# One program part for experts and final sum, with the last four experts' results moved on TensorE

## What is computed

```python
logits = jnp.einsum('bsd,ed->bse', x, gate_w) + gate_b
probs = jax.nn.softmax(logits, axis=-2)
vals_t, idx_t = jax.lax.top_k(probs.transpose(0, 2, 1), K)
...
merged = jnp.einsum('bked,bke->bed', tok, vals)
...
h = jnp.einsum('bei,eih->beh', jnp.concatenate([merged, ones], -1), w1)
h = jax.nn.gelu(h, approximate=False)
o = jnp.einsum('bej,ejo->beo', jnp.concatenate([h, ones], -1), w2)
out_tok = jnp.einsum('beo,bke->bkeo', o, vals).reshape(b, K * E, d)
out = jnp.zeros_like(x).at[jnp.arange(b)[:, None], flat_idx].add(out_tok)
```

## Time and profile before

| | us |
|---|---|
| median of three runs (lowest, highest) | 877.07 (875.35, 880.38) |
| the profiled execution's own time | 874.81 |
| its span | 873.1 |
| TensorE busy (matmuls) | 706.8 |
| DVE busy | 614.8 |
| ACT busy | 355.5 |
| GpSimd (POOL) busy | 452.6 |

### The profile page before, as it was taken

How to read it: one execution, slowest core, us unless ns; L and a number is a source line. 1 busy time by engine, 2 the same in 40 slices (tenths; PEclk the granted TensorE clock), 3 DMA queues, 4 the chain that set the end, 5 groups by cost and what they waited for, 6 DMA issues and landing times. The chain is left out here.

```text
span 873.1 us, 20447 instructions
## 1 busy us (share of the span) xinstructions
PE 706.8 (81%) x7708; PEld 475.9 (55%) x7708; DVE 614.8 (70%) x889; ACT 355.5 (41%) x561; POOL 452.6 (52%) x257
## 2 busy tenths in 40 slices
PE   4566759886899999999999999994899859976774
PEld 3354534444677777777776777773677523322231
DVE  3599947888999999999999999993477520100014
ACT  2366635443445544455444545542555321210000
POOL 1598700001999999999999999993122000000000
PEclk9799979998999999999999999996999959889685
DMA  5100000000001010000000000001930188999987
GB/s 111 49 2 0 0 1 0 0 0 14 8 15 38 14 33 9 12 12 12 12 8 11 12 12 12 14 15 56 389 100 1 40 346 341 412 413 421 413 350 247
DMA packets 49211, 86.34 MB, mean 99 GB/s; under 512 B 5552, under 2 KB 32752, under 8 KB 49168
## 3 DMA queue, kind: packets, MB, share of 16 engines
q1 hardware_dynamic: 45616, 83.33, 26.1%
q10 hardware_dynamic: 3552, 2.43, 0.9%
HBM read 76.31 MB, written 9.44 MB: 98 GB/s over the span
## 5 line engine op out<-in xcount | busy, mean ns | idle before, releaser
L898 POOL TENSOR_TENSOR read<-state,q_pos 128x1024 f32<-128x1024 f32 x128 | 300.4, 2365 | 28.7 <-DVE state L1007 22.4
L1007 DVE TENSOR_TENSOR_SCAN state<-fac,ps_up 128x1024 f32<-128x1024 f32 x128 | 290.0, 2277 | 8.6 <-ACT fac L942 8.6
L942 ACT ACTIVATE fac<-ps_xf 128x1016 f32<-128x1016 f32 x128 | 130.2, 1018 | 176.3 <-PE ps_xf L1041 159.9
L1041 PE MATMUL ps_xf<-hot,xtab 64*128 64x128 f32 x2048 | 148.4, 284 | 11.0 <-ACT fac L942 8.9
L1041 PEld LDWEIGHTS ps_xf<-hot,xtab 64*128 64x128 f32 x2048 | 125.4, 188 | 58.0 <-ACT fac L942 43.8
L1041 PE MATMUL ps_up<-hot,utab 64*128 64x128 f32 x2048 | 139.9, 276 | 19.5 <-DVE state L1007 19.5
L1041 PEld LDWEIGHTS ps_up<-hot,utab 64*128 64x128 f32 x2048 | 126.4, 189 | 25.1 <-issue 17.8
L907 POOL TENSOR_TENSOR utab<-tab 128x1024 f32 (+1 forms) x32 | 64.5, 2016 | 93.8 <-SPq L85 93.8
L1086 PE MATMUL ps_o<-read,sel 128*32 128x256 f32 x1024 | 82.7, 395 | 3.7 <-POOL read L898 3.7
L1637 DVE COPY h_t<-ps_ht 128x512 f32<-128x512 f32 x16 | 10.3, 686 | 75.5 <-PE ps_ht L1666 75.4
L997 DVE TENSOR_TENSOR xtab<-tab,ps_k 128x1024 f32<-128x1024 f32 x64 | 59.5, 929 | 1.5 <-PE ps_k L1033 1.5
(11 more groups left out here) (199 smaller groups left out, 987.7 us busy)
## 6 DMA issues: line engine op xcount, KB each, us to landing
w_sb<-in_L_ffn_w SPq DMA_DIRECT2D x32, 2048.0 KB, 20.1
rec_out<-osb SPq DMA_DIRECT2D x128, 32.0 KB, 1.5
ao<-rec_out SPq DMA_DIRECT2D x8, 512.0 KB, 4.1
out_dram<-h SPq DMA_DIRECT2D x8, 256.0 KB, 2.5
out_dram<-h ACTq DMA_DIRECT2D x8, 256.0 KB, 3.1
tok<-in_x SPq DMA_DIRECT2D x2, 512.0 KB, 10.6
exp_out<-eo SPq DMA_DIRECT2D x8, 128.0 KB, 18.6
oq<-exp_out SPq DMA_DIRECT2D x8, 128.0 KB, 2.9
```

The lines of the kernel that those rows point to most:

```text
L898: nc.gpsimd.tensor_tensor(read[n % 2][:], state[n % 4][:].rearrange("p (b i t) -> p b i t", b=2, i=IB), q_pos[x.s][:, :, x.k].unsqueeze(2) ...
L942: nc.scalar.activation(fac[n % 2][:].rearrange("p (n t) -> p n t", t=T)[:, :, 1:], ps_x[:].rearrange("p (n t) -> p n t", t=T)[:, :, 1:], A ...
L1007: nc.vector.tensor_tensor_scan(state[n % 4][:], fac[n % 2][:], ps_u[n % 2][:], 0.0, ALU.mult, ALU.add)\
L1041: last = nc.tensor.matmul(dst[:, b * 512 + col * T:b * 512 + (col + 1) * T], stationary[rows], pos[rows], start=True, stop=True)
```

## The change

Experts and combine become one program part, and the parts share one Chain semaphore for DVE and one for GpSimd. The last four experts (set 7, LAST = 28 on) no longer go through DRAM:

- At the start GpSimd builds strip, from which picks_of_last takes selectors: TensorE, between first_layer(0, 0) and first_layer(0, 1), brings the last four experts' picks of quad q to partitions 32j + 8x + q, with zeros on the strip's other partitions, and DVE copies them to last_picks.
- At the end rows_of_last puts the last result (128 rows in eo) on the same partitions with four matmuls, and DVE copies them to last_rows.
- Set 6's result is stored from ACT's queue. ACT then waits for that store and for those of sets 0 to 5 (set 5's is still in SP's queue, after the last w2 loads), and issues the reload: four transfers of 28 partitions by eight quads, 224 KB each.
- The sum of a quad is now eight matmuls: four over 28 partitions, picks times oq, and four over 32, last_picks times last_rows.

PSUM is one tensor of eight banks, used by both stages. In the diff below, the other places where a chain's own semaphore gives way to the shared one are left out, as are lines that only move.

```diff
 HT = HID // P
+LAST = X - QB
 EPS = 1e-5
...
-        m = {"start": start}
+        m = {"start": start, "vch": Chain(nc.vector, sem("v_chain")), "pch": Chain(nc.gpsimd, sem("p_chain"))}
...
             recurrent_outputs(nc, a, m, sem, lambda n, s, d=F32: sb(mid, n, s, d), replace_tables)
-        m["oq"] = sb(life, "oq", [P, QUADS, E])
         with ExitStack() as last:
-            experts(nc, a, m, sem, lambda n, s, d=F32: sb(last, n, s, d))
-        combine(nc, m, sem, out)
+            experts(nc, a, m, sem, lambda n, s, d=F32: sb(last, n, s, d), out)
...
-            ch = Chain(dve, vch)
+            ch = m["vch"]
...
-        pch, ch = Chain(nc.gpsimd, sem("p_chain1")), Chain(nc.vector, sem("v_chain5"))
+        pch, ch = m["pch"], m["vch"]
...
-def experts(nc, a, m, sem, sb):
-
-    ident, merged, exp_out, oq = m["ident"], m["merged"], m["exp_out"], m["oq"]
+def experts(nc, a, m, sem, sb, out):
+
+
+    ident, merged, exp_out, h2, picked = m["ident"], m["merged"], m["exp_out"], m["h2"], m["picked"]
     w1, w2, b1, b2, w1_ld, w2_ld = m["w1_sb"], m["w2_sb"], m["b1_sb"], m["b2_sb"], m["w1_ld"], m["w2_ld"]
...
     eo = sb("eo", [P, 2, E])
+    oq = sb("oq", [P, QUADS, E])
+    last_rows = sb("last_rows", [P, E])
+    last_picks = sb("last_picks", [P, QUADS, T])
+    strip = sb("strip", [P, QUADS + X])
...
     with ExitStack() as ctx:
-        ps_1 = [ctx.enter_context(nc.psum_tensor(f"ps_1{s}", [P, HID], F32)) for s in range(2)]
-        ps_t = ctx.enter_context(nc.psum_tensor("ps_ht", [P, HT, P], F32))
-        ps_2 = [ctx.enter_context(nc.psum_tensor(f"ps_2{s}", [P, 512], F32)) for s in range(2)]
+        ps = ctx.enter_context(nc.psum_tensor("ps_e", [P, 8, 512], F32))
+        ps_1 = [ps[:, 2 * s:2 * s + 2].rearrange("p n c -> p (n c)") for s in range(2)]
+        ps_t = ps[:, 4:6].rearrange("p n (h q) -> p (n h) q", q=P)
+        ps_2 = [ps[:, 6 + s] for s in range(2)]
+        ps_q = [ps[:, 4 * s:4 * s + 4] for s in range(2)]
+        ps_p = ps[:, 4, 0:E]
...
         mq_ok, gl, ht, htok, eo_ok = (sem(n) for n in ("mq_ok", "gl", "ht", "htok", "eo_ok"))
-        l1, l2, eo_st, f_ld = ([sem(f"{n}{s}") for s in range(2)] for n in ("l1_", "l2_", "eo_st", "z_ld"))
-        m["f_ld"] = f_ld
+        l1, l2, eo_st, f_out = ([sem(f"{n}{s}") for s in range(2)] for n in ("l1_", "l2_", "eo_st", "z_out"))
+        sp_ok, lp_mm, lp_ok, lr_mm, lr_ok, f_ld, f_mm, f_add = (
+            sem(n) for n in ("sp_ok", "lp_mm", "lp_ok", "lr_mm", "lr_ok", "z_ld", "z_mm", "z_add"))
+        dst = out.rearrange("(q p s) t e -> q s t p e", s=2, p=2)
+
+        def store_rows(eng, s):
+            for q in range(QUADS):
+                eng.wait_ge(f_add, START + q + 1)
+                eng.dma_start(dst[q, s], h2[:, QB * q + 2 * s:QB * q + 2 * s + 2]).then_inc(f_out[s], 16)
+            eng.wait_ge(f_out[s], START + 16 * QUADS)
+
+        def store_results(eng, i, s):
+            q = 2 * i + s
+            eng.wait_ge(eo_ok, START + q + 1)
+            eng.dma_start(exp_out[bass.ds(QB * q, QB)].rearrange("x b e -> (x b) e"), eo[:, s]).then_inc(eo_st[s], 16)
         TURNS = X // QB // 2
...
             for s in range(2):
                 hidden(TURNS - 1, s)
 
+            store_results(act, TURNS - 1, 0)
+            act.wait_ge(eo_st[0], START + 16 * TURNS)
+            act.wait_ge(eo_st[1], START + 16 * (TURNS - 1))
+            src = exp_out.rearrange("x (q j) e -> j x q e", j=QB)
+            for j in range(QB):
+                act.dma_start(oq[j * X:j * X + LAST], src[j, 0:LAST]).then_inc(f_ld, 16)
+            store_rows(act, 1)
+
+        @block.gpsimd
+        def _(pool):
+            pch = m["pch"]
+            cols = strip[:].rearrange("p (x q) -> p q x", q=QUADS)[:, QUADS - 1, 0:QB]
+            pch.link(nc.gpsimd.memset(strip[:], 0.0))
+            pch.link(nc.gpsimd.tensor_tensor(cols, ident[:, LAST:X], ident[:, X + LAST:2 * X], ALU.add))
+            pch.link(nc.gpsimd.tensor_tensor(cols, cols, ident[:, 2 * X + LAST:3 * X], ALU.add))
+            nc.gpsimd.tensor_tensor(cols, cols, ident[:, 3 * X + LAST:4 * X], ALU.add).then_inc(sp_ok, 1)
+
         @block.sync
         def _(sp):
             m["start"](sp)
-
-            def store(i, s):
-
-                q = 2 * i + s
-                sp.wait_ge(eo_ok, START + q + 1)
-                sp.dma_start(exp_out[bass.ds(QB * q, QB)].rearrange("x b e -> (x b) e"),
-                             eo[:, s]).then_inc(eo_st[s], 16)
-
-            def reload(h):
-
-                quads = slice(h * QUADS // 2, (h + 1) * QUADS // 2)
-                src = exp_out.rearrange("x (q j) e -> j x q e", j=QB)
-                for j in range(QB):
-                    sp.dma_start(oq[j * X:(j + 1) * X, quads], src[j][:, quads]).then_inc(f_ld[h], 16)
...
                 for h in range(2):
                     sp.wait_ge(l2[s], START + 2 * i - 1 + h)
                     load_w2(sp, a, QB * (2 * i + s), h, w2[s], w2_ld[s])
-                store(i - 1, s)
+                store_results(sp, i - 1, s)
...
             for s in range(2):
                 second_weights(TURNS - 1, s)
-            for s in range(2):
-                store(TURNS - 1, s)
-            for s in range(2):
-                sp.wait_ge(eo_st[s], START + 16 * TURNS)
-            for h in range(2):
-                reload(h)
+            store_rows(sp, 0)
 
         @block.vector
         def _(dve):
+            dve.wait_ge(lp_mm, START + 1)
+            nc.vector.tensor_copy(last_picks[:], ps_t).then_inc(lp_ok, 1)
...
                     nc.vector.tensor_copy(eo[:, s], ps_2[s][:, 0:E]).then_inc(eo_ok, 1)
+
+            dve.wait_ge(lr_mm, START + 1)
+            nc.vector.tensor_copy(last_rows[:], ps_p).then_inc(lr_ok, 1)
+            for q in range(QUADS):
+                dve.wait_ge(f_mm, START + q + 1)
+                rows = h2[:, QB * q:QB * (q + 1)]
+                nc.vector.tensor_tensor(rows, ps_q[q % 2][:, :, 0:E], rows, ALU.add).then_inc(f_add, 1)
...
+            def picks_of_last():
+
+                pe.wait_ge(sp_ok, START + 1)
+                for q in range(QUADS):
+                    at = QUADS - 1 - q
+                    for j in range(QB):
+                        rows = slice(j * X, (j + 1) * X)
+                        last = nc.tensor.matmul(ps_t[rows, q], strip[rows, at:at + X], picked[rows, q],
+                                                start=True, stop=True)
+                last.then_inc(lp_mm, 1)
+
+            def rows_of_last():
+
+                pe.wait_ge(eo_ok, START + 2 * TURNS)
+                for j in range(QB):
+                    last = nc.tensor.matmul(ps_p[j * X:(j + 1) * X],
+                                            ident[:].rearrange("p (n j) -> p j n", j=QB)[:, j],
+                                            eo[:, 1], start=True, stop=True)
+                last.then_inc(lr_mm, 1)
+
+            def output(q):
+                pe.wait_ge(f_add, START + q - 1)
+                for j in range(QB):
+                    rows = slice(j * X, j * X + LAST)
+                    nc.tensor.matmul(ps_q[q % 2][:, j, 0:E], picked[rows, q], oq[rows, q], start=True, stop=False)
+                if q == 0:
+                    pe.wait_ge(lr_ok, START + 1)
+                for j in range(QB):
+                    rows = slice(j * X, (j + 1) * X)
+                    last = nc.tensor.matmul(ps_q[q % 2][:, j, 0:E], last_picks[rows, q], last_rows[rows],
+                                            start=False, stop=True)
+                last.then_inc(f_mm, 1)
+
             pe.wait_ge(m["wbias"], START + 32)
 
             first_layer(0, 0)
+            picks_of_last()
             first_layer(0, 1)
+            pe.wait_ge(lp_ok, START + 1)
             transpose_hidden(0, 0)
             second_layer(0, 0)
...
             transpose_hidden(TURNS - 1, 1)
             second_layer(TURNS - 1, 1)
-
-
-def combine(nc, m, sem, out):
-
-    h2, picked, oq, f_ld = m["h2"], m["picked"], m["oq"], m["f_ld"]
...
-    with ExitStack() as ctx:
-        ps = [ctx.enter_context(nc.psum_tensor(f"ps_fo{s}", [P, QB, 512], F32)) for s in range(2)]
-        block = ctx.enter_context(nc.Block())
-        f_mm, f_add, f_out = sem("z_mm"), sem("z_add"), [sem(f"z_out{s}") for s in range(2)]
-        dst = out.rearrange("(q p s) t e -> q s t p e", s=2, p=2)
-
-        def stores(eng, s):
+            rows_of_last()
+            pe.wait_ge(f_ld, START + 16 * QB)
             for q in range(QUADS):
-                eng.wait_ge(f_add, START + q + 1)
-                eng.dma_start(dst[q, s], h2[:, QB * q + 2 * s:QB * q + 2 * s + 2]).then_inc(f_out[s], 16)
-            eng.wait_ge(f_out[s], START + 16 * QUADS)
-
-        @block.sync
-        def _(sp):
-            m["start"](sp)
-            stores(sp, 0)
-
-        @block.scalar
-        def _(act):
-            stores(act, 1)
-
-        @block.tensor
-        def _(pe):
-
-            for q in range(QUADS):
-                if q % (QUADS // 2) == 0:
```

(25 more changed lines are left out.)

## The result

| | before | changed |
|---|---|---|
| median of 17 runs each, us | 877.80 (874.74 to 880.38) | 881.12 (879.05 to 884.52) |
| ratio to before, 95% interval | | 1.0045 [1.0032, 1.0058] |
| profiled execution: span, us | 873.1 | 878.4 |
| experts' start (ACT's first copy of mq), us | 714.56 | 717.24 |

The mean of the three is 0.35%, 3.1 us. The forecast was 1.8 us in the other direction, and its range ended at 879.0: it was wrong in sign and size.

A forecast was written before the change was run, and what follows sets the result against it. The weight stream was taken to bound the experts, the stores the output stage. First add 2.06 us earlier, plus 0.25 of starved stores, gave -1.8 us: 875.3 us against a median of 877.07; range 871.5 to 879.0.

The forecast's parts named there:

- When the reload starts: End of the experts: the reload waits for the sixth store, behind the last weights; first issue at 850.0.
- How long it takes: Reload, first issue to first output matmul: 0.92 MB, 4.9 us in sum, so TensorE starts at 854.9.
- Rival 3: Reload: slices of 28 partitions use the DMA engines worse, +0.5 us, 875.8; chance 0.15.
- The first quad: Output stage: sixteen matmuls instead of eight, 2.09 us at half clock, 0.81 per further eight.
- The stores run on: Output stage: stores are the bound; the end follows the first add by 12.8 us if adds keep pace.
- the second quad: Output stage: its add follows 1.62 us after the first, against the stores' 1.37, starving them 0.25 us.
- The common chain semaphores: Semaphores shared across program parts: same waits, other numbers; 0, with 0.5 us either way.
- The picks, POOL's part, the block boundary: Experts' start and block boundary: no cost; picks take 2.56 us, hidden in 4.4 us of slack.
- rival 4: Experts' start: picks_of_last starves the weight stream past 4.4 us; 879.6, or 888.3 at half clock; chance 0.07.

The follow-up runs named there:

- shared_chains: The kernel before with only the common chain semaphores of the change; ratio to before 1.001.
- reload_32: The changed kernel with each of the four reloads taking 32 partitions instead of 28; ratio to before 1.0028.
- fetch_earlier: The changed kernel with 32 small unused matmuls more on TensorE while it waits for the reload; ratio to before 1.0026.
- sum_twice: The kernel before with each quad's four output matmuls done twice, same result; ratio to before 1.0026.
- halves_warm: The changed kernel, reload in two halves, TensorE waiting for the first, and 32 unused matmuls in the wait for the last w2 half; ratio to before 0.9982.
- halves_warm_plus1: halves_warm with the scaling of the class counts cut into two DVE instructions; 872.57 us, ratio to before 0.9938.
- changed_third: The changed kernel unaltered, run once more as the yardstick of later runs on the same chip; ratio to before 1.0037.
- before_plus1: The kernel before with the scaling of the class counts cut into two DVE instructions instead of one; one execution, its time not counted.
- after_again: The changed kernel unaltered, run once more for a second trace; ratio to before 1.0024.

## Why the prediction was wrong, step by step

- **When the reload starts: right.** 850.0 was said, that is 135.4 us after the experts' start; 135.2 to 135.6 in the three traces of the changed kernel. In the two traces of the kernel before it was 138.8 and 140.0, so the gain is 3.6 us in the first pair and 4.3 on average over five traces of either kind (with shared_chains and the kernels with added DVE instructions); it was put at 3.4. The sixth store landed behind the weights (852.34, that is 135.1 us after the start), as said.
- **How long it takes: failed, the largest error.** "Sum 4.9, so TensorE starts at 854.9" measured 7.5. The bytes were counted rightly (0.92 MB, against the 0.81 MB that the old reload had moved in its wait). Three other parts of the sum were too short. Nothing moves in the first 1.6 us after the first issue (up to 854.0), where the old reload had 0.6: 1.0 us more. The 0.92 MB then take 5.0 us at 183 GB/s, where 4.1 was said: 0.9 more. And TensorE starts only 1.0 us after 859, with 5 GB/s moving in between (0.03 of the engines), where the sum had nothing. The old wait ended with the first half's landing while the second half still moved, so no such end showed there; a wait for all of a transfer has one. The estimate of 250 GB/s "once the stream is up" was true of the old reload (251 from 855 to 858), but the new one did not exceed 224 in any microsecond. The issues of 28 partitions took 0.82 us (the first 1.46) where 0.47 was taken. How much of the late start and of the low rate they cause is open: reload_32 with issues of 0.62 to 0.70 gained nothing, but moved 14% more. Against before the term is +3.2 us, where +0.5 was said. Rival 3 named the place and its mark of 5.5 us was passed, but its price was 0.5 us.
- **The first quad: right**, +0.84 us in the first pair, where 0.81 was said.
- **The stores run on, "provided that later adds come at least every 1.37 us": failed.** Additions did come often enough (1.71 us from the first to the second, where 1.62 was said, then 1.2 to 1.3; 1.31 on average), and the clock came back 4.4 us after the first output matmul, where 4 were said. The Trainium skill, "TensorE: Matmul & The Clock Gate", "What's actually happening", has sustained activity lift the throttle; the trace agrees, with a granted clock of 0.81 from 864 to 865 and 1.00 after it, TensorE having run almost without a gap since 859.96. Yet the tail was 15.1 us where "12.8 to 13.1" was said. What the forecast lacked is that TensorE's longer program needs another 16 KB of code just then, fetched by DMA among the stores. With the matmuls doubled and the fetch ahead of the stores, the tail is 13.0 to 13.4 (fetch_earlier, sum_twice, halves_warm, halves_warm_plus1), that is 0.2 to 0.6 us over before, about the 0.25 that the forecast had for the second quad; with the fetch among them it is 14.4 to 15.3. That the fetch makes the tail is shown by moving it; that the last stores wait behind it on the one engine is the likely way, and argued.
- **"The common chain semaphores … 0, with 0.5 us either way": mis-sized, and for another reason.** +1.0 us, not from the waits (the kernel before gets it too, with one elementwise instruction more and its own chains) but from where the loop comes to lie.
- **The picks, POOL's part, the block boundary: right**, nothing on the path; rival 4 fell with 1.95 us against 4.4 us of slack.

On average over five traces of either kind the terms are -4.3 (earlier issue) + 3.1 (reload) + 0.9 (first quad) + 2.1 (tail) + 1.0 (loop) = +2.8 us, against 3.1 measured. A single term varies by up to 1.7 us from trace to trace, so the agreement is no closer than that. With the forecast's own numbers in place of the reload's and the tail's (+0.5 and +0.25) it would have been -1.7, close to the -1.8 that was said. That closeness is luck in part: the gain was put 0.9 us too low, and the loop's 1.0 us was left out.

Open is a difference of 2 us in the stage before the experts: from the last scan to the experts' start some executions take 126 us and others 128, where eight matmuls of L1419 run at half clock (3.67 us for the eight in the changed kernel, 1.89 otherwise). It occurs with either kernel (126.1 in changed_third, 128.0 in before_plus1), so it is not counted to the change. The long form is in two of the six traces built on the kernel before and in eight of the thirteen built on the changed one, too few to settle whether the change makes it more frequent. halves_warm's trace has it and halves_warm_plus1's has not, so it may be part of what the latter gained.

## What to carry to other kernels

When a wait is moved, ask what it now waits for: four transfers of all the quads start earlier, but the first consumer needs half of them, and cutting them in two won back all that the change had cost (3.5 to 4.4 us). Size a transfer by the bytes that its consumer waits for and a rate that the same kind of transfer has shown in the same place, and add what passes before the first bytes move and after the last. A stage that is bound by DMA can be disturbed by the fetching of the code that its own engines run: look for instruction packets among the data before believing that it goes on unchanged.

## What the runs showed of the hardware that was not expected

- A 16 KB fetch of program code takes 1.1 us of one engine with little beside it (7.0% of sixteen in a microsecond, fetch_earlier at 861), and 1.2 to 2.0 us among stores (7.3% in after_again, 12.5% in changed_third). With it among the stores, the slowest of sixteen 256 KB stores landed after 4.7 to 5.8 us instead of 3.4 to 3.5.
- Reloading rows of 1 KB from DRAM moved between 130 GB/s (the changed kernel at 855) and 265 (the kernel before at 855) within a microsecond in mid-stream, and 224 to 236 at a share of 1.0 or more (reload_32), where the stores of the output stage move 383.
- One DVE instruction more or less ahead of a loop is worth 1.0 us in six passes here (0.4 in the first, 0.12 in each later one), and the wait moves between neighbouring instructions as more are added.
- 32 unused matmuls in a wait of 3.5 us kept TensorE at full clock, and the 32 instructions after it took 1.93 us in all three kernels that had them, where the others took 2.45 to 3.64.
